# Aggregates over 32 destination groups at a time, in two passes over even and odd source tiles, with the counts stored as two halves

## The reference, cut to what matters

```python
def _aggregate(x, src, dst, num_nodes):
    return jax.ops.segment_sum(x[src], dst, num_segments=num_nodes)
...
h = _aggregate(x, src, dst, num_nodes)      # layer 1
h = jax.nn.relu(h)
h = _aggregate(h, src, dst, num_nodes)
...
msg = h[src] * norm[:, None]                # layer 2, four times
out = jax.ops.segment_sum(msg, dst, num_segments=n)
```

## Time and profile before

| what | us |
|---|---|
| median of 3 runs (lowest, highest) | 6171.97 (6163.17, 6188.61) |
| the profiled execution, its own time | 6197.27 |
| its span, first to last instruction | 6195.5 |
| busy: PE matmuls, PE weight loads | 3670.3, 2190.1 |
| busy: DVE, ACT, POOL | 2485.6, 1530.3, 3155.6 |

### The profile page before, as it was taken

One profiled execution on the slowest core, in us unless ns is written; L12 is line 12 of the kernel. 1 busy time (PEld: TensorE's weight loads), 2 busy tenths in 40 slices (PEclk: granted clock), 3 DMA queues, 4 the chain that ended last, 5 costly groups with the idle time before them and its releaser, 6 DMA issues.

```text
span 6195.5 us, 94079 instructions
## 1 busy us (share of the span) xinstructions
PE 3670.3 (59%) x23495; PEld 2190.1 (35%) x23496; DVE 2485.6 (40%) x7582; ACT 1530.3 (25%) x3833; POOL 3155.6 (51%) x3156
## 2 busy tenths in 40 slices
PE   5377777777777777778244444254454434445647
PEld 2143443334333334334133333133233223323435
DVE  5265665666566665666401200310120021021088
ACT  3132232223232232323112111021111111111157
POOL 0455555555555555553565655655535545544610
PEclk8588788888888888888566666576566666657778
DMA  5333333333333333332233333243223323313556
GB/s 178 79 77 75 81 80 75 76 76 79 80 77 76 76 79 76 80 77 65 70 122 140 125 120 134 73 150 121 87 96 121 124 88 138 117 40 131 153 191 237
DMA packets 505437, 641.28 MB, mean 104 GB/s; under 512 B 323429, under 2 KB 380099, under 8 KB 499054
## 3 DMA queue, kind: packets, MB, share of 16 engines
q1 hardware_dynamic: 342845, 489.07, 23.7%
q0 software_dynamic: 101760, 110.75, 8.6%
q10 hardware_dynamic: 60720, 40.23, 2.0%
HBM read 446.94 MB, written 189.43 MB: 103 GB/s over the span
## 4 chain that ended last, share of the span: by engine, by line
PE 45%; issue 25%; another core or an unknown queue 11%; DVE 8%; DMA 7%; ACT 2%; DVEq 1%; SPq 0%; ACTq 0%
PE bank L1736 12%; PE bank L1659 10%; PE bank L1660 7%; PE bank L1664 7%; DMA rel_and_z<-adjacency 2%; PE bank L1690 2%; DMA ld_all<-adjacency 2%; DMA rel_table<-ld_all 1%; PE bank L1852 1%; PE bank L1696 1%; DMA ld_all<-l_sorted 1%; DVE hid_T L1501 1%; PE bank L1688 1%; PE bank L1786 1%
## 5 line engine op out<-in xcount | busy, mean ns | idle before, releaser
L659 POOL DMA_INDIRECT l_sorted<-arena,l_pos x1568 | 1610.7, 1027 | 1413.3 <-ACT arena L794 943.5
L644 POOL DMA_INDIRECT ld_all<-rel_table,rel_and_z x1564 | 1539.7, 984 | 1337.5 <-issue 585.6
L1659 PE MATMUL bank<-hid_T 128*128 128x400 f16 x2346 | 953.7, 407 | 562.2 <-issue 480.0
L1736 PE MATMUL bank<-ld_all 128*128 128x256 fp8e4 (+1 forms) x3822 | 622.5, 313 | 682.8 <-issue 589.6
L1660 PE MATMUL bank<-hid_T 128*128 128x384 f16 x2346 | 928.1, 396 | 27.9 <-issue 26.8
L1257 DVE TENSOR_SCALAR hid_T<-count_key,hid_T 128x400 f16<-128x400 int16 x2346 | 588.8, 321 | 762.2 <-remote 483.9
L1736 PE MATMUL bank<-rel_and_z,ld_all 128*128 128x256 fp8e4 x3528 | 514.4, 291 | 490.0 <-issue 449.9
L1197 DVE COPY accT<-bank 128x256 f32<-128x256 f32 (+1 forms) x150 | 62.2, 415 | 1849.3 <-remote 1350.8
L1736 PEld LDWEIGHTS bank<-ld_all 128*128 128x128 f16 x3822 | 403.1, 111 | 894.8 <-issue 819.3
L1659 PEld LDWEIGHTS bank<-hid_T 128*128 x2346 | 253.9, 108 | 1035.2 <-issue 1030.3
L1664 PE MATMUL bank<-ld_all,arena 128*32 x4692 | 533.4, 251 | 123.9 <-issue 122.1
(11 more groups left out here) (258 smaller groups left out, 3986.9 us busy)
## 6 DMA issues: line engine op xcount, KB each, us to landing
ld_all<-adjacency SPq DMA_DIRECT2D x72, 1568.0 KB
rel_and_z<-adjacency SPq DMA_DIRECT2D x72, 1568.0 KB
l_sorted<-zeros SPq DMA_DIRECT2D x147, 424.0 KB
arena<-in_edge_attr SPq DMA_DIRECT2D x195, 256.0 KB
ld_all<-l_sorted SPq DMA_DIRECT2D x33, 1277.5 KB, 6.0
adjacency<-ld_all ACTq DMA_DIRECT2D x391, 98.0 KB
rel_table<-ld_all SPq DMA_DIRECT2D x49, 520.0 KB, 3.3
l_sorted<-arena,l_pos POOLq DMA_INDIRECT x1568
```

What stands on the lines that cost most here:

```text
L644: pool.indirect_dma_start(ring[:, c % RING, 0:TW], None, rel_table, bass.IndirectOffsetOnAxis(ap=rel_i[:, c:c + 1], axis=0)).then_inc(s(f" ...
L659: pool.indirect_dma_start(l3_sorted, bass.IndirectOffsetOnAxis(ap=l3_pos[0:parts, n * SB_K + k:n * SB_K + k + 1], axis=0), rows16[q][0:par ...
L1659: pe.matmul(b0[:, 0:w0], low[:, 0:P], pair_hot[q % 2][:, k, 0:w0], start=k == 0, stop=k == CG - 1)
L1736: ins = pe.matmul(bank[slot][:, 0:n * GN].rearrange("p (g d) -> p g d", d=GN), x16[:, t, :], a_half[slot][:, 0:n, place(t) * GN:(place(t) ...
```

## The change

The unit of an aggregate becomes 32 groups, 512 columns, one whole PSUM bank, in 13 windows instead of 25 halves. A window is made in two pieces (`side`): 25 matmuls over the even source tiles, then 24 over the odd ones, which add up in the same bank. The counts in DRAM get a dimension `o` for even and odd, and each half of a row is padded to 400 bytes (`HW` words). Buffer 0 holds even counts of a window, buffer 1 the odd ones. SP loads a side again when PE has signalled the same side of the window before. DVE and ACT take windows (512 and 256 columns at once) on every second step, and the splits of the edge blocks are tied to sides in place of halves, again three to a block.

```diff
@@ -33,7 +33,7 @@
 CG = 6
 A_SPLIT = 25
 GW = SRC_T * GN
-HG = 16
+HG = 32
...
-        adjacency = dram("adjacency", [-(-NG // TG) * P * TG, GW // 4])
-        adjacency_row = adjacency.rearrange("(b p q) f -> p b q f", p=P, q=TG)
-        adjacency_block = adjacency.rearrange("(b p q) f -> p b (q f)", p=P, q=TG)
+        adjacency = dram("adjacency", [-(-NG // TG) * 2 * P * TG, HW])
+        adjacency_row = adjacency.rearrange("(b o p q) f -> p b q o f", o=2, p=P, q=TG)
+        adjacency_block = adjacency.rearrange("(b o p q) f -> p b o (q f)", o=2, p=P, q=TG)
...
-        half_words = [t[:, 0:HG * GW // 4] for t in (ld_all[:, NT * D:2 * NT * D], rel_and_z[:, :])]
+        half_words = [t[:, 0:HG * HW] for t in (ld_all[:, NT * D:2 * NT * D], rel_and_z[:, :])]
         a_half = [t.bitcast(f8).rearrange("p (g f) -> p g f", g=HG) for t in half_words]
...
+                        words, blocks = n * HW, -(-n // TG)
                         sp.wait_ge(s("half_mm"), used)
-                    coming = [(m, m % 2, NH * a + m + 1) for m in range(0 if a == 0 else 2, NH)]
+                        sp.dma_start(half_words[side][:, 0:words].rearrange("p (b f) -> p b f", b=blocks),
+                                     adjacency_block[:, at * (HG // TG):at * (HG // TG) + blocks, side, 0:words // blocks]).then_inc(s(f"half_in{side}"), 16)
...
+                    coming = [(m, side, 2 * (NH * a + m) + side + 1) for m in range(0 if a == 0 else 1, NH) for side in range(2)]
                     if a < 5:
-                        coming += [(1, 1, NH * (a + 1) + 1), (0, 0, NH * (a + 1) + 2)]
+                        coming += [(0, side, 2 * NH * (a + 1) + side + 1) for side in range(2)]
+                    for at, side, used in coming:
+                        half(at, side, used)
                         halves += 1
                         if halves % 3 == 1 and coming_block <= NSB:
                             block_in(coming_block)
...
-                act.dma_start(adjacency_row[:, bass.ds(b, 1), q, :], count_words.unsqueeze(1)).then_inc(s("counts_stored"), 16)
+                act.dma_start(adjacency_row[:, bass.ds(b, 1), q, :, :], count_words.rearrange("p (a o f) -> p a o f", a=1, o=2)).then_inc(s("counts_stored"), 16)
...
                         act.wait_ge(s("half_fin"), m + 3)
-                        act.copy(G[:, tiles, :], bank[2 + slot][:, 0:2 * D].rearrange("p (t d) -> p t d", d=D)).then_inc(s("half_out"), 1)
-                    for i in range(NH):
-                        m = NH * a + i
+                        act.copy(G[:, t0:t0 + n, :], bank[2 + slot][:, 0:n * D].rearrange("p (t d) -> p t d", d=D)).then_inc(s("half_out"), 1)
+                    for i in range(2 * NH):
+                        m = 2 * NH * a + i
                         blk = 2 + m // 3
                         if m % 3 == 0 and blk <= NSB:
                             split_middle(blk)
                         if m % 3 == 1 and blk <= NSB:
                             split_low(blk)
-                        out(m, i % 2, slice(2 * i, 2 * i + 2))
+                        if i % 2:
+                            out(m // 2, i // 2 % 2, i // 2 * (HG // TG), min(HG // TG, SRC_T - i // 2 * (HG // TG)))
                         if m % 3 == 2 and blk < NSB:
                             split_high(blk + 1)
...
-                    for i in range(NH):
-                        m, slot, n = NH * a + i, i % 2, min(HG, NG - i * HG) * GN
-                        v.wait_ge(s("half_mm"), m + 3)
-                        v.wait_ge(s("half_fin"), m + 1)
-                        if n < HG * GN:
-                            v.memset(accT[slot][:, n:HG * GN], 0)
-                        v.tensor_copy(accT[slot][:, 0:n], bank[slot][:, 0:n]).then_inc(s("acc_read"), 1)
+                    for i in range(2 * NH):
+                        m, slot, n = 2 * NH * a + i, i // 2 % 2, min(HG, NG - i // 2 * HG) * GN
+                        if i % 2:
+                            v.wait_ge(s("half_mm"), m + 3)
+                            v.wait_ge(s("half_fin"), m // 2 + 1)
+                            if n % P:
+                                v.memset(accT[slot][:, n:-(-n // P) * P], 0)
+                            v.tensor_copy(accT[slot][:, 0:n], bank[slot][:, 0:n]).then_inc(s("acc_read"), 1)
                         blk = 2 + m // 3
                         if m % 3 < 2 and blk <= NSB:
                             split_less(blk, m % 3)
...
+                link(v.memset(count_words[:, GW // 4:2 * HW], 0))
...
-                    def place(t):
-                        return t // 2 + HI * (t % 2)
-
                     def multiply(m, slot, loads, n=HG):
 
-                        pe.wait_ge(s(f"half_in{slot}"), loads)
-                        pe.wait_ge(s("acc_read"), m + 1)
-                        pe.sem_inc(s("turn"), 1)
-                        for t in range(SRC_T):
-                            ins = pe.matmul(bank[slot][:, 0:n * GN].rearrange("p (g d) -> p g d", d=GN), x16[:, t, :],
-                                            a_half[slot][:, 0:n, place(t) * GN:(place(t) + 1) * GN], start=t == 0, stop=t == SRC_T - 1)
-                        ins.then_inc(s("half_mm"), 1)
-
-                    def finalize(m, slot):
+                        for side in range(2):
+                            pe.wait_ge(s(f"half_in{side}"), loads)
+                            if side == 0:
+                                pe.wait_ge(s("acc_read"), m + 1)
+                            pe.sem_inc(s("turn"), 1)
+                            for t in range(side, SRC_T, 2):
+                                ins = pe.matmul(bank[slot][:, 0:n * GN].rearrange("p (g d) -> p g d", d=GN), x16[:, t, :],
+                                                a_half[side][:, 0:n, t // 2 * GN:(t // 2 + 1) * GN], start=t == 0, stop=t == SRC_T - 2)
+                            ins.then_inc(s("half_mm"), 1)
+
+                    def finalize(m, slot, tiles=HG // TG):
 
                         pe.wait_ge(s("acc_read"), m + 3)
                         pe.wait_ge(s("half_out"), m + 1)
-                        for q in range(2):
+                        for q in range(tiles):
                             ins = pe.matmul(bank[2 + slot][:, q * D:(q + 1) * D], accT[slot][:, q * P:(q + 1) * P], unscale[:],
                                             start=True, stop=True)
                         ins.then_inc(s("half_fin"), 1)
 
-                    m0, in0, in1 = NH * a, (NH // 2 + 1) * a, NH // 2 * a
-                    multiply(m0, 0, 16 * (in0 + 1))
+                    m0, rest = NH * a, NG - (NH - 1) * HG
+                    multiply(m0, 0, 16 * (m0 + 1))
                     with pe.Fori(0, NH // 2 - 1) as i:
-                        multiply(i * 2 + (m0 + 1), 1, i * 16 + 16 * (in1 + 1))
+                        multiply(i * 2 + (m0 + 1), 1, i * 32 + 16 * (m0 + 2))
                         finalize(i * 2 + m0, 0)
-                        multiply(i * 2 + (m0 + 2), 0, i * 16 + 16 * (in0 + 2))
+                        multiply(i * 2 + (m0 + 2), 0, i * 32 + 16 * (m0 + 3))
                         finalize(i * 2 + (m0 + 1), 1)
-                    multiply(m0 + NH - 2, 1, 16 * (in1 + NH // 2))
+                    multiply(m0 + NH - 2, 1, 16 * (m0 + NH - 1))
                     finalize(m0 + NH - 3, 0)
-                    multiply(m0 + NH - 1, 0, 16 * (in0 + NH // 2 + 1), NG - (NH - 1) * HG)
+                    multiply(m0 + NH - 1, 0, 16 * (m0 + NH), rest)
                     finalize(m0 + NH - 2, 1)
-                    finalize(m0 + NH - 1, 0)
+                    finalize(m0 + NH - 1, 0, -(-rest // TG))
```

More of the change, by code:

```diff
@@ L59 @@
 HI = 25
+HW = HI * GN // 4
 STARTS_AFTER = 40
@@ L255, in build @@
         at += 2 * NG
-        count_words = ld_all[:, at:at + GW // 4]
+        count_words = ld_all[:, at:at + 2 * HW]
         count_stage = count_words.bitcast(f8)
-        at += GW // 4
+        at += 2 * HW
         over_junk = ld_all[:, at:at + GW // 2].bitcast(f16)
@@ L518, in _, with half @@
                 with sp.If(flag2):
-                    def half(at, slot, used):
+                    def half(at, side, used):
                         n = min(HG, NG - at * HG)
-                        words, blocks = n * GW // 4, -(-n // TG)
+                        words, blocks = n * HW, -(-n // TG)
                         sp.wait_ge(s("half_mm"), used)
-                        sp.dma_start(half_words[slot][:, 0:words].rearrange("p (b f) -> p b f", b=blocks),
-                                     adjacency_block[:, at * (HG // TG):at * (HG // TG) + blocks, 0:words // blocks]).then_inc(s(f"half_in{slot}"), 16)
-                    coming = [(m, m % 2, NH * a + m + 1) for m in range(0 if a == 0 else 2, NH)]
+                        sp.dma_start(half_words[side][:, 0:words].rearrange("p (b f) -> p b f", b=blocks),
```

(11 more changed lines are left out.)

3 lines of the change are left out of this document (1 added, 2 removed).

## The result

The change moved the median from 6168.93 us (20 runs, 6140.19 to 6204.76) to 6139.28 us (20 runs, 6092.88 to 6171.69), a ratio of 0.9935 with a 95% interval of 0.9916 to 0.9954. That is 30 us less, where 163 were forecast. The profiled execution took 6145.23 us, its span 6143.5.

The account below looks back on a forecast made before the run. PE, slowed while POOL scatters, and POOL were taken to go in step, with pauses between blocks. Pauses -174, layers +6, loads +5 gave -163 us: 6197.3 to 6034 profiled, median 6009; likeliest range 5920 to 6080, whole 5890 to 6150.

Parts of the forecast that it names:

- The pattern: In the aggregates, POOL's scatter blocks follow each other in pairs, with one pause near 18 us for each pair.
- The second block's supply: In a pair's second scatter block PE runs 30 matmuls in 40.4 us; 37 of 171 are missing and bring the pause.
- the store: Outstanding PE work in the aggregates, counted in instructions, that empties slowly while POOL scatters and at once when it rests.
- Its length is that of the long one, 17.5: A pair's one pause behind two scatter blocks: 17.5 us, plus 1.0 for evacuations and later signals, 18.5 for 26.4.
- The sum: Whole kernel: -174 from POOL's pauses, +6 layers, +5 loads, -163 us in all.
- I take 6, near the lower: Layers between aggregates: larger first and last units cost 6 us, within bounds of 0 to 33.
- Count stage 0: Count stage: the smaller 400 byte store pieces stay hidden beside other work and cost 0 us.
- Loads and evacuations: Aggregates: 156 loads for 150 cost 5 us (bounds 0 to 100); wider copies on DVE and ACT cost nothing.
- (1): Rival, aggregates: every scatter block keeps a 9.6 us pause, 159 us less, 6024 us; chance 0.16.
- (2): Rival, aggregates: POOL never rests, all 581 us of pauses go, 5602 us; chance 0.05.
- (3): Rival, aggregates: columns or time limit PE, 52 wide matmuls a block, pauses stay, 6183 us; chance 0.13.
- (4): Rival, count stage: small stores cost 1 us a group, 391 us less the 163 gained, 6400 us; chance 0.08.

Follow-up runs that it names:

- e14: Changed kernel run again without an edit, on a chip of the slower level: 6142.59 us, 1.0004 of the kernel before.
- e13: Changed kernel with six chained memsets on POOL, a 6 us rest, behind each block of 32 scatters; slower-level chip: 5800.07 us, 0.9462 of the kernel before.
- e11: Kernel before with the last two parts of edge block 27 issued ahead of the first dense layer; slower-level chip: 6141.63 us, 1.0025.
- e10: Kernel before with its edge blocks tied to 26 steps an aggregate; faster-level chip: 4836.61 us, 1.0081 of the kernel before.
- e12: Changed kernel with edge blocks tied to 25 of 26 sides and block 27's last parts ahead of the first dense layer; slower-level chip: 6136.11 us, 1.0017.

## Why the prediction was wrong

The pattern was right (pairs, one pause for two blocks, 29 waits for 47, a count stage of the same length). The direction was right in the first comparison (0.9935), but not in e14 on another chip of kind B (1.0004), so it owes something to luck. The size was wrong, by two steps: the pauses fell by 77 us and not 174, and half of what POOL gained did not reach the end.

*The second block's supply.* "In the second block nothing has emptied the store, and I take the slow rate: 23 in 30.9 us, 30 in 40.4." It got 13 to 15. The first block gave what it needed (93 and 91; 104 was only a ceiling of 85.5 wanted), so 65 were missing and not 37, and the pauses became 24.6 to 26.5 us instead of 18.5. The second term of the same step failed with it, "Its length is that of the long one, 17.5, as ACT is then a whole split behind": the delay is 9.1 us for 4.8, and ACT, done with its subtractions, waits for PE's load, side and finalize. A nearer row was at hand: the kernel before does 5 in the last 10.4 us of a block, which would have given 19 and not 30. e13 shows the cause on the same kind of chip: with 6 us of rest the supply is back, and 342 us go. The store of some 80 to 90 quick matmuls, narrow or wide, isn't refuted (93 and 91 in a first block, before 106, and 79 at the very start after 61 us of scatters); what was wrong is a constant rate behind it. Whether that rate falls by time or by what PE has issued the runs don't separate. The rows lean to the number: 30 us behind a rest 100 narrow and 91 wide matmuls have passed, though the wide ones came later (17 in the third stretch, before 7).

*What sets the end.* The sum took POOL's pauses for the time. POOL's pauses, with those under a microsecond, fell from 841.8 to 765.0 us: the three long ones grew from 260 to 291 (71.7, 93.9, 125.6), the rest fell from 581 to 474, where 407 were forecast. Its scatters took 20 us less, and it ended 97 us sooner. But the last output came only 48 us sooner (5886.4, now 5838.4), and behind it lie 309 and 305 us of the kernel's end. The four other traces of chip B with all scatters (e11 to e14) have 302 to 309 us there as well, so in both kernels the last output sets the end, and not POOL. Before, that output came 22 us ahead of POOL's end; now it comes 27 behind. The profiled execution thus gained 52 us; the medians differ by 30, because that of the kernel before lay 28 us under its profiled execution and that of the changed kernel 6. The step was "I take 6, near the lower" for the layers: the aggregates' ends are tied to whole blocks by the 26 parts, which stood in the change and which I did not count. That this costs time is shown on chip A (e10, 38 us); for chip B it is argued. There e12, with one more edit, brings the last output of the second aggregate from 3994.9 to 3929.4 us and yet gains nothing by its median; so what held the last output back by 49 us on chip B stays open.

*The rest of the terms.* Count stage 0: no loss can be seen on chip B (last store at 2957.7 and 2957.8 us); 11 us on chip A. The Trainium skill (DMA: Bandwidth & Descriptors, Specifications) asks for at least 512 bytes a transfer for line rate. The traces show no such penalty by itself: the packets of ACT's queue went from 60720 to 110768 and their share of 16 engines' span from 2.0% to 2.5%, so the queue costs a quarter more and not three times as much. Loads and evacuations: not told apart in the time.

*The rivals.* (1) fell, since pauses of 0.3 us are there. (2) fell. (3) fell in its form, as 93 wide matmuls pass in a block and not 52; so nearly as many wide matmuls pass in a block as narrow ones (106 and 102). (4) fell on chip B: no cost of 0.42 us a group.

*The premise behind all of it.* On chip A the same program runs without slow stretches, 1370 us faster, and there the change costs 1.0%. The prediction speaks of chip B alone. Why the kinds differ is not settled: the count of instructions (94079), the bytes moved (641.28 MB) and the 40.4 us of a block are the same.

No version beats both kernels everywhere. e13 does on chip B (0.9462) and costs 5.7% on chip A.

## What to carry to other kernels

A rate taken as the mean of a stretch in which it still falls is too high for whatever comes after that stretch: cut the stretch in four and use the last. When work is tied to steps of another loop, recount the ties after the number of steps changes (here 25 to 26), since one tie too many puts off an end by a whole unit of the slower engine. A pause's length is set by the last thing in it, so follow each engine of the pause to its end before giving it a price. And a kernel that is measured on one chip only may be tuned to that chip's limit.

## What the runs showed of the hardware

- One program runs at two levels on chips of one model: the kernel before takes 4795 to 4798 us on four, 6126 to 6169 where the rest was measured. A block of 32 scatters takes 40.4 us at both. The count stage differs too (last store at 2334 and 2958 us).
- While GpSimd issues indirect scatters on chip B, TensorE falls from 46 or 80 matmuls in 10 us to 4 or 5 after 30 us, at the lower level of its clock (granted 0.50), and the records of fp32 matmuls come 2.80 us apart. Signals reach the other engines late: a window whose last matmul ended at 4193.6 us was copied by DVE at 4244.9, 51 us later, after an idle wait. A GpSimd busy with memsets for 6 us is rest enough (e13).
- A rest costs most of its length where it isn't needed: on chip A 49 rests of 6 us (294 in all) add 222 us, of 3 us (147) 122 us.
